# Macaron attention: the mask in quadrants, value products directly after the scores, value projection first

## What is computed

```python
qkv = shift_token(x) @ wqkv
q, k, v = heads of qkv
q, k = rotary_xpos(l2norm(q) * q_scale, l2norm(k) * k_scale)
sim = 8 * q @ k.T                      # 64 queries against their own and the previous 64 keys
sim = where(mask, -big, sim)           # mask: later keys, keys over 64 back, keys before the start
x = x + softmax(sim) @ v @ wo
h = layernorm(shift_token(x)) @ w1 + b1
x = x + (a * gelu(g)) @ w2 + b2        # a, g: the halves of h
```

## Time and profile before

| | |
|---|---|
| median of three runs | 2216.92 us (2213.29 to 2218.58) |
| span of the profiled execution | 2218.2 us (no other time is recorded for it) |
| TensorE matmuls busy | 1862.6 us, 84% |
| VectorE, ScalarE, GpSimd busy | 1573.0, 1392.0 and 1284.7 us (71, 63 and 58%) |
| the two macaron phases | from 772 to 1397 us and from 1552 to 2186 us |

### The profile page before, as it was taken

One profiled execution on the slowest core, in us unless ns is written; L12 is line 12 of the kernel. 1 busy time (PEld: TensorE's weight loads), 2 busy tenths in 40 slices (PEclk: granted clock), 3 DMA queues, 4 the chain that ended last, 5 costly groups with the idle time before them and its releaser, 6 DMA issues. The chain is left out here.

```text
span 2218.2 us, 51508 instructions
## 1 busy us (share of the span) xinstructions
PE 1862.6 (84%) x16704; PEld 1411.6 (64%) x16705; DVE 1573.0 (71%) x2848; ACT 1392.0 (63%) x3948; POOL 1284.7 (58%) x1099
## 2 busy tenths in 40 slices
PE   4169957716996699999999999675899999999996
PEld 4158842515884377777777776342677777777774
DVE  4548858644886588878778887243788878788883
ACT  5125543212554478887888877365688788878874
POOL 4354410246442587878878786101887878778771
PEclk9979979657997699999999999787999999999999
DMA  6212140021214211101011010000111111110111
GB/s 202 68 58 61 44 108 15 18 75 59 66 44 113 74 25 28 24 21 28 21 28 25 21 27 18 4 0 3 33 24 23 24 23 28 25 25 21 26 23 38
DMA packets 87308, 88.26 MB, mean 40 GB/s; under 512 B 13978, under 2 KB 65863, under 8 KB 87016
## 3 DMA queue, kind: packets, MB, share of 16 engines
q1 hardware_dynamic: 77288, 68.09, 12.1%
q0 software_dynamic: 8704, 17.85, 2.4%
q10 hardware_dynamic: 1152, 0.25, 0.1%
HBM read 35.60 MB, written 22.22 MB: 26 GB/s over the span
## 5 line engine op out<-in xcount | busy, mean ns | idle before, releaser
L2037 POOL TENSOR_TENSOR mac_probs<-mac_probs,mac_prec 128x512 f32<-128x512 f32 x256 | 265.5, 1043 | 204.4 <-DVE mac_prec L1852 203.6
L1713 ACT ACTIVATE mac_probs<-banks,mac_nmax 128x128 f32<-128x128 f32 x1024 | 359.6, 386 | 0.2
L1809 DVE TENSOR_TENSOR route_pool<-banks,tables 128x1024 f32<-128x1024 f32 x256 | 301.0, 1217 | 36.2 <-ACT route_pool L1673 31.7
L2017 POOL TENSOR_TENSOR route_pool<-route_pool 128x1024 f32<-128x1024 f32 x128 | 303.2, 2369 | 39.0 <-DVE route_pool L1809 15.8
L1843 DVE TENSOR_REDUCE mac_nmax<-banks 128x4 f32<-128x512 f32 x256 | 164.9, 686 | 139.0 <-PE banks L1541 139.0
L2028 POOL TENSOR_TENSOR mac_qkn<-route_pool,mac_rc 128x1024 f32<-128x1024 f32 x128 | 243.9, 1905 | 16.6 <-issue 7.6
L854 POOL DMA_INDIRECT x_sorted<-route_pool,route_index x128 | 124.5, 973 | 217.1 <-DVE route_index L666 122.7
L862 POOL DMA_INDIRECT y_tokens<-moe_bench,moe_goal x144 | 140.9, 979 | 178.9 <-DVE moe_bench L805 132.2
L1713 ACT ACTIVATION_READ_ACCUMULATOR mac_probs<-banks,mac_nmax 128x1 f32 x1024 | 231.8, 226 | 0.0
L54 PE MATMUL banks<-wqkv_h,mac_hh 128*128 128x512 f32 x384 | 179.8, 468 | 26.4 <-POOL mac_hl L1992 21.4
L388 PE MATMUL banks<-w,moe_gh 128*128 x576 | 163.3, 360 | 44.9 <-issue 26.9
(11 more groups left out here) (315 smaller groups left out, 5069.1 us busy)
## 6 DMA issues: line engine op xcount, KB each, us to landing
mac_v_even<-mac_v SPq DMA_DIRECT2D x224, 128.0 KB, 2.2
moe_xs<-x_sorted SPq DMA_DIRECT2D x144, 72.0 KB
route_pool<-y_tokens SPq DMA_DIRECT2D x16, 512.0 KB, 7.2
y_tokens<-moe_bench,moe_goal POOLq DMA_INDIRECT x144, 2.3
moe_bench<-in_L_attn_x SPq DMA_DIRECT2D x8, 256.0 KB, 5.4
route_pool<-in_L_ffn_W SPq DMA_DIRECT2D x4, 512.0 KB, 7.0
x_sorted<-route_pool,route_index POOLq DMA_INDIRECT x128
b<-in_b_flat SPq DMA_DIRECT2D x1, 2048.0 KB
```

What stands on the lines that cost most here:

```text
L1713: e = act.activation(probs[:, r, p, :], m.ps[:, S + r, p * P:(p + 1) * P], ACT.Exp, bias=nmax[:, r, p:p + 1], accum_out=psum[:, r, p:p + 1])
L1809: turn = dve.tensor_tensor(turned[:, i, :, :].rearrange("q k (h s j) -> q k h s j", s=2, j=DH // 2), q[:, :, :, ::-1, :] if i else q, tabl ...
L2017: pool.tensor_tensor(sums[:], turned[:, 0, :, :], turned[:, 1, :, :], ALU.add).then_inc(added, 1)
L2037: pool.tensor_tensor(probs[:, r, :, :], probs[:, r, :, :], prec[:, r, :].unsqueeze(2).to_broadcast([P, HP, P]), ALU.mult).then_inc(shared[ ...
```

## The change

The order on four engines is changed, and the mask product is cut up. On TensorE: the products with the values stand directly behind the scores and ahead of the transposes of queries and keys; the three projections come in the order values, keys, queries (before: keys, queries, values), with the `centre` and `up` between the first and the second as before; the mask product of 64 rows by 128 columns, one for each r, becomes two of 64 by 64 for each r; a wait moves ahead, and in t = 0 a bare increment of a new semaphore, for which nobody waits, is added. On ScalarE `keep_kt(n+2)` goes behind `exps(n+1, 1)`. On VectorE `keep_qt(n+1)` goes behind `norms` and `reciprocals(n, 1)`. On GpSimd `await_upper` waits for the count of query and key projections, which now come last, rather than for the values'.

```diff
+        ready, sim_done, ... = sem("ready"), sem("sim_done"), ...
...
                 if which == 2:
+                    if t % 2 == 0:
+                        pe.wait_ge(split, START + 2 * j + t // 2 + 1)
                     pe.wait_ge(v_kept, START + k)
...
-                if which == 1 and t % 2 == 0:
-                    pe.wait_ge(split, START + 2 * j + t // 2 + 1)
...
+                pe.wait_ge(zeroed, START + 2)
                 if live(n - 1):
                     for r in range(H2):
                         pe.wait_ge(pt_kept[r], START + n)
                 pe.wait_ge(qt_kept, START + n + 1)
                 pe.wait_ge(kt_kept, START + n + 1)
-                pe.wait_ge(zeroed, START + 2)
-                for r in range(H2):
-                    rows = slice(DH * r, DH * r + DH)
-                    pe.matmul(m.ps[:, S + r, :], m.both_bf[rows, :], m.masks[rows, 0, :], start=True, stop=True)
+                if t == 0:
+                    pe.sem_inc(ready, 1)
+                for k in range(2):
+                    for r in range(H2):
+                        rows, at = slice(DH * r, DH * r + DH), slice(k * WIN, (k + 1) * WIN)
+                        pe.matmul(m.ps[at, S + r, :], m.both_bf[rows, at], m.masks[rows, 0, :], start=True, stop=True)
...
                     sims(n, t)
+                    values(n - 1, *before)
                     turn_qk(n + 1, (t + 1) % NT)
                     if t == 0:
                         up(i - 2, lay, 0, 2, F, gated, MC * (i - 2) + 1)
                     if t == 2:
                         down(i - 2, lay)
-                    values(n - 1, *before)
-                    project(n + 3, *ahead, lay, 1)
+                    project(n + 3, *ahead, lay, 2)
                     if t == 1:
                         centre(i - 1)
                     if t == 3:
                         up(i - 1, lay, 0, 0, F, gelued, MC * (i - 1) + 1)
+                    project(n + 3, *ahead, lay, 1)
                     project(n + 3, *ahead, lay, 0)
-                    project(n + 3, *ahead, lay, 2)
                     turn_probs(n, 1)
...
+                    exps(n + 1, 1)
                     keep_kt(n + 2, (t + 2) % NT)
-                    exps(n + 1, 1)
...
                     maxima(n, 0)
-                    keep_qt(n + 1)
                     norms(n + 2)
                     reciprocals(n, 1)
+                    keep_qt(n + 1)
...
-                    pool.wait_ge(v_projected, START + NT * (j - 1) + 2 * (s + 1))
+                    pool.wait_ge(qk_projected, START + 2 * (NT * (j - 1) + 2 * (s + 1)))
```

More of the change, by code:

```diff
@@ L1465, in macaron_phase @@
         q_turned, k_turned, qt_kept, kt_kept = sem("q_turned"), sem("k_turned"), sem("qt_kept"), sem("kt_kept")
-        sim_done, maxed = sem("sim_done"), [sem(f"maxed{r}") for r in range(H2)]
+        ready, sim_done, maxed = sem("ready"), sem("sim_done"), [sem(f"maxed{r}") for r in range(H2)]
         exped, recip = [sem(f"exped{r}") for r in range(H2)], [sem(f"recip{r}") for r in range(H2)]
```

## The result

The changed kernel takes 2234.56 us (median of four runs, 2225.14 to 2238.0) where the kernel before takes 2216.26 (four runs, 2213.29 to 2218.58): 18.3 us more, ratio 1.0081 with a 95% interval of 1.0065 to 1.0096. It is slower by 0.8%. The forecast was 2220, with a range of 2195 to 2242 and the same chance for either sign; the time lies in the range. It is near the value of the rival in which GpSimd holds t = 1 and 3 (2239), but not by that rival's sum: that one has 0.70 us an item, and the item grew by 0.26. The profiled execution of the changed kernel spans 2236.2 us, that of the kernel before 2218.2.

What follows compares the result with a forecast made beforehand. Bounds were taken per step: TensorE's order in t = 0, 1 and 3, the queries' projection in t = 2. Terms 0.31 - 0.31 + 0.39 - 0.31 + 0.03 = +0.11 us an item, times 32 = +3.5, gave 2220.4 us; range 2195 to 2242.

Steps and rivals of the forecast that it cites:

- the rival in which GpSimd holds t = 1 and 3: Share not ready for the earlier transposes, both gains lost: 0.70 us an item, +22 us, 2239; chance 0.12.
- The mask: Mask product in quadrants on TensorE: gain of 0.12 us in t = 1, 2, 3 and 0.08 in t = 0.
- The switch of form: Value products behind the scores save a form change before them: 0.19 us in t = 1, 3, 0.20 in t = 0, 2.
- t = 2, +0.39: Step t = 2: square follows the later query projection, at 1026.30 instead of 1025.91, with ScalarE's chain behind it: 0.39 us longer.
- t = 3, -0.31: Step t = 3: shorter by TensorE's saving of 0.31 us; square's path comes to the same time within 0.02.
- t = 0, +0.31: Step t = 0: square 0.39 us later behind the queries, next mask at 1009.24 instead of 1008.93.
- PE's own order gates, with the copy 0.08 behind: End of t = 0, kernel before: TensorE's order sets the next mask's start, ScalarE's last copy 0.08 us behind.
- From square to the end of the second copy 2.23: ScalarE in t = 0: fixed 2.23 us, plus 0.11 to TensorE, added to the later square to place the next mask.
- t = 1, -0.31: Step t = 1: transposes 0.31 us earlier, at 1016.44, with GpSimd's share and the load still before them.
- this shifts with the step's start too: Argument against the GpSimd rival: add, ahead of share in t = 1, hangs on rotate and square, but shifts with the step.
- Times 32: Both macaron phases: one item's change, +0.11 us, times 32 items gives the whole, +3.5 us.
- The pattern repeats ... in 128 steps: Both phases: first mask products show step lengths within 0.1 us of the chosen item's in 128 steps, 32 items' worth.

## Why the prediction came out as it did

The direction had no favourite (0.36 for faster, 0.36 for slower). The forecast itself, 3.5 us more, was the likeliest case (0.46, within 12 us) and fell short by 14.8 us; the time is inside the stated range because the range is wide. By the prediction's own sign the mechanism is wrong in one place, for t = 1 did not shrink, and it is GpSimd's first share that ends the wait of its transposes. Step by step:

- **The mask**: forecast 0.12 us a step, 0.08 in t = 0; the run of it alone measured 0.11, 0.08, 0.14 and 0.14 in t = 0 to 3, against the steps of the kernel before on the first chip. Right, with all of the 0.15 between mask and transposes; in t = 1 only 0.08 came through, since GpSimd's first share gates there once TensorE is that much earlier.
- **The switch of form**: forecast 0.19 to 0.20; shown as 0.16 to 0.19 in t = 0, 2 and 3. Right.
- **t = 2, +0.39**: measured +0.39, by the mechanism given; the run with the old projection order in t = 2 took it away.
- **t = 3, -0.31**: measured -0.33. Right.
- **t = 0, +0.31** (0.34 with the increment): measured +0.07. Two steps failed. "PE's own order gates, with the copy 0.08 behind" is incomplete for the kernel before: its last transposes start 0.05 us behind the end of the second share, so GpSimd's share gates as much, and it does not move earlier with TensorE. And "From square to the end of the second copy 2.23" held waits for the transposes; with the transposes ready it is 2.00 (1005.42 to 1007.42), which puts the next mask at 6.45 + 2.00 + 0.11 = 8.56 us into the step, no later than the share does. The share I had put at nothing: ScalarE's 0.08 behind keep_kt reach it through exps(0) and the reciprocal (it ends 0.07 later). keep_kt alone is 0.17 there.
- **t = 1, -0.31**: failed, measured +0.14. The step is "share ended at 1016.08 ... still before it", with "this shifts with the step's start too" among the rivals. 1016.08 is the end of the second share; the one that counts is the first, and it left TensorE's order only 0.12 us to gain. And the addition does not shift with the step's mask but with the square. I had made the mask follow the square by a fixed 2.34, so the two shifted together on paper; the mask came 0.23 us earlier than that, while the addition, GpSimd's pieces behind it and the transposes stood with the square. The rival named the right place, with the right lever (share later by over 0.1 relative to its step; it was 0.34 in the step shown and 0.23 in the mean); its price, 0.31 in both t = 1 and 3, fitted neither: t = 1 lost 0.45 against the forecast and t = 3 kept its gain.
- **Times 32**: "the price of the change is that of one item times 32" failed. The item's +0.26 gives 8 us of 18. "The pattern repeats ... in 128 steps" was a misreading: in the trace of the kernel before, the first item of a phase takes 34.3 us and the second 37.4, and the first and the last step 9.1 and 12.4, and a drain follows. Restoring the old orders in the unrolled end items gave 10 to 11 us back. Two parts of the order's loss there are in the traces: transposes in the first step wait 2.08 us for rotate (0.67 before), whose square now stands behind three projections instead of two; and in the drain the last up product stands behind value products that wait, 1.4 us a phase. The other part, some 7.5 us between the two profiled executions, lies in stretches of the same work that ran at the lower clock. Whether the change makes such stretches likelier stays open: they also occur in variants whose ends have the order of the kernel before, and no run held the clock fixed.

So the two errors of the item, -0.27 in t = 0 and +0.45 us in t = 1, cancelled in part: the item's +0.11 was near the measured +0.26 by luck as much as by reading, and the total missed what lies outside the steady items.

## What to carry to other kernels

An interval taken from a trace (square to last copy) may hold waits that the change removes; write it as work plus waits before you add it to a moved start. When a start is moved within a pipeline, every chain hanging on it keeps its own clock: list them all (here copies, rotate, addition, GpSimd) and compare each with the new step's start, not with the old. Where a wait comes in parts (two shares, two groups of transposes), compare each part with what needs it: the first can gate while the last has room. And an in-order schedule that is tuned per step deserves an experiment per step: here the best order differed from t to t, and taking the best of each beat both kernels. Cost the fill and the drain separately from the loop, and compare their clocks before you blame the order.

## What the runs showed of the hardware

- Four 64 by 64 mask products start as one group (four loads in 0.11 us), and the scores behind them in the same form follow without a hole; behind a 64 by 128 mask there were 0.23 us idle.
- The last step of a phase took 12.41 and 13.89 us in one execution of the changed kernel, with a granted clock of 1.00 and 0.88. Over the 28 phases of the 14 traces its clock was below full in 15, in variants with either order of the ends. Ahead of the slower stretch TensorE stood idle for 1.72 us, and it did so in the fast case too.
- The same holds behind the last mask: the same `centre`, `variance` and down products took 1.12, 1.13 and 2.82 us at a granted clock of 1.00, and 2.08, 2.07 and 4.74 at 0.51. Together with the last steps this moved one execution against another by some 7.5 us of 2200, of the size of the change's own loss in the steady items.
